# A routed expert layer on one core: routing by halves, one-hot matrices in batches, and later reads of the second matrices

## The reference

```python
w = weights[conditions]
y = jnp.einsum('bct,bcd->bdt', x, w)
probs = softmax(xt @ w_router)              # xt: y as (1024, 256), 16 experts
top_w, top_i = top_k(probs, 4);  top_w = top_w / sum(top_w)
g = silu(xt @ we1[e]) * (xt @ we3[e]) * cw[:, e]
moe_out = sum over e of g @ we2[e]
shared = silu(xt @ ws1) * (xt @ ws3) @ ws2
out = x + shared / 5 + moe_out * 4 / 5
```

## Time and profile before

| | us |
|---|---|
| median of 3 runs | 150.36 |
| lowest and highest | 146.83, 150.56 |
| the profiled execution | 146.87 |
| its span, first to last instruction | 145.0 |
| TensorE, VectorE, ScalarE, GpSimd busy | 133.6, 103.3, 78.9, 66.3 |

### The profile page before, as it was taken

The page is one execution under the profiler, slowest core; times in us unless marked ns, Lnnn a source line. Parts: engine busy times, 40 slices in busy tenths (PEclk is TensorE's granted clock), DMA queues, the critical chain, the costliest instruction groups (busy, mean ns, idle before and its releaser), DMA issues.

```text
span 145.0 us, 2785 instructions
## 1 busy us (share of the span) xinstructions
PE 133.6 (92%) x786; PEld 112.0 (77%) x786; DVE 103.3 (71%) x290; ACT 78.9 (54%) x193; POOL 66.3 (46%) x79
## 2 busy tenths in 40 slices
PE   5999999989798999999999999899999999999470
PEld 2347997778487788999898889798999888888350
DVE  1301879998828999877879887887888653066992
ACT  4003637999404986677586777447945321107900
POOL 0700000002765687778776566577777777000000
PEclk9999999999999999999999999999999999999998
DMA  2823898989952232365437322122222222399924
GB/s 43 288 60 80 239 255 291 341 250 285 368 189 75 77 98 83 112 183 181 152 107 204 124 101 92 66 113 109 109 106 87 101 109 112 85 392 411 374 77 145
DMA packets 17549, 24.18 MB, mean 167 GB/s; under 512 B 3424, under 2 KB 14304, under 8 KB 17408
## 3 DMA queue, kind: packets, MB, share of 16 engines
q1 hardware_dynamic: 13440, 14.23, 30.1%
q0 software_dynamic: 3120, 8.52, 16.6%
q10 hardware_dynamic: 976, 1.26, 2.6%
HBM read 17.58 MB, written 6.42 MB: 166 GB/s over the span
## 4 chain that ended last, share of the span: by engine, by line
PE 61%; DVE 21%; DMA 7%; issue 5%; ACT 3%; DVEq 1%; ACTq 0%
PE up_ps L1004 17%; PE down_ps L1022 11%; PE down_ps L920 8%; PE gate_ps L907 5%; PE up_ps L907 4%; PE up_ps L998 4%; PE gate_ps L957 4%; PE down_ps L982 3%; PE down_ps L862 2%; DMA itok_rows<-in_itok_B 2%; DMA g<-in_L_cond_weights,cond_idx 2%; DVE g L632 2%; ACT w_hi L468 2%; DVE raw L805 2%; DVE x_lo L764 2%
## 5 line engine op out<-in xcount | busy, mean ns | idle before, releaser
L444 POOL DMA_INDIRECT result<-store_t,back_i x32 | 31.3, 979 | 12.9 <-issue 6.7
L437 POOL DMA_INDIRECT xt<-y_of,token_i x16 | 16.3, 1019 | 35.0 <-DVE token_i L716 28.1
L798 DVE SCALAR_TENSOR_TENSOR store_t<-down_ps,valid,store_t 128x256 f32 x47 | 21.7, 461 | 8.7 <-DVE store_t L798 5.8
L1004 PE MATMUL up_ps<-w_hi,x_hi 128*128 x78 | 23.8, 305 | 1.1 <-DVE x_lo L764 0.9
L1022 PE MATMUL down_ps<-w,gt 128*128 x94 | 24.5, 381 | 0.0
L1004 PE MATMUL up_ps<-w_lo,x_hi 128*128 x78 | 22.1, 283 | 0.0
L1004 PE MATMUL up_ps<-w_hi,x_lo 128*128 x78 | 22.0, 282 | 0.0
L437 POOL DMA_INDIRECT raw<-y_of,token_i x16 | 15.8, 985 | 4.9 <-issue 4.0
L1022 PEld LDWEIGHTS down_ps<-w,gt 128*128 128x128 f32 x94 | 16.0, 190 | 1.7 <-issue 0.5
L1004 PEld LDWEIGHTS up_ps<-w_hi,x_hi 128*128 128x128 f32 x78 | 14.8, 190 | 2.5 <-issue 2.4
L764 DVE TENSOR_TENSOR x_lo<-store_t,x_hi 128x256 fp32r<-128x256 f32 x39 | 14.8, 421 | 0.6 <-ACT x_hi L536 0.3
(11 more groups left out here) (156 smaller groups left out, 260.0 us busy)
## 6 DMA issues: line engine op xcount, KB each, us to landing
raw<-in_L_ffn_we SPq DMA_DIRECT2D x30, 128.0 KB, 3.3
w<-in_L_ffn_we SPq DMA_DIRECT2D x4, 512.0 KB, 6.4
w_lo<-result SPq DMA_DIRECT2D x4, 512.0 KB, 6.7
raw<-result SPq DMA_DIRECT2D x4, 512.0 KB, 7.0
acc<-in_x SPq DMA_DIRECT2D x2, 512.0 KB, 4.6
y_of<-store_t ACTq DMA_DIRECT2D x1, 1024.0 KB, 6.0
out<-acc SPq DMA_DIRECT2D x3, 256.0 KB, 2.2
xt<-in_L_ffn_ws SPq DMA_DIRECT2D x4, 128.0 KB, 2.7
```

The lines of the kernel that those rows point to most:

```text
L437: pool.indirect_dma_start(rows_of(p)[:, j % 2, :], None, y_of, bass.IndirectOffsetOnAxis(ap=token_i[:, j:j + 1], axis=0),).then_inc(tile_i ...
L444: pool.indirect_dma_start(result, bass.IndirectOffsetOnAxis(ap=back_i[:, j:j + 1], axis=0), merged[:, j, :], None,).then_inc(result_out[j ...
L798: dve.scalar_tensor_tensor(out=into, in0=out_ps[n % 2][:, h, :], scalar=valid[:, it:it + 1], in1=into, op0=ALU.mult, op1=ALU.add).then_inc ...
L1004: last = pe.matmul(gu_ps[b][:, h, :], (x_hi, x_lo)[a][:, b, h, k * P:(k + 1) * P], pair_of(w, experts[h], k), start=(m == 0), stop=(m == 3 ...
```

## The change

1. **y's rows.** ScalarE copies y a second time as `y_f`, in float32, a piece at a time, between `y_hi` and the splits; `token_rows` turns these pieces back with 16 transposes.
2. **Routing by halves.** The searches and the comparison that makes `pick` are done per half, with `low(0)` in the first; `top_d` goes behind the mask, and its exponential on ScalarE behind three more splits. TensorE does a half gate product ahead of the ranks.
3. **One-hots.** `tile_hot`, `row_hot` and `dest_hot` are laid out with the pair's number n innermost, their inputs are bfloat16, and constants `count_tile`, `count_row` (1,024 elements each) and `count_n` are made at the start. `rows_hot` does one comparison of 1,024 elements in place of eight. `dest_hot` has two planes, not three: the partition (one copy on ScalarE) and n (one product on VectorE). `back_i` is made first, and `token_i` is its upper bits. The matmuls of `choices` have 64 columns and read both operands with a step.
4. **Second matrices.** SP waits for the first four gathers before it issues `w_2`; TensorE's wait for it moves from ahead of the first turn to the first product that reads it.

```diff
@@ views
+        y_f = store_t[:, 0:TT, :].rearrange("p t d -> p (t d)").rearrange("p (k n) -> p k n", k=KD)
-        row_hot = early(16, 8).bitcast(BF16).rearrange("p (n r) -> p n r", r=P)
-        tile_hot = early(24, 2).bitcast(BF16).rearrange("p (n j) -> p n j", j=TILES)
-        dest_hot = early(26, 6).bitcast(BF16).rearrange("p (n m j) -> p n m j", m=3, j=TILES)
+        row_hot = early(16, 8).bitcast(BF16).rearrange("p (c r n) -> p c r n", c=TOP_K, n=TT)
+        tile_hot = early(24, 2).bitcast(BF16).rearrange("p (j n) -> p j n", n=TK)
+        dest_hot = early(26, 4).bitcast(BF16).rearrange("p (m j n) -> p m j n", m=2, n=TK)
...
@@ sync
+            for j in range(2 * RING - 2):
+                sp.wait_ge(tile_in[j], 16)
             for q in range(4):
...
                 sp.dma_start(w_2[:, e, :], we2[e].rearrange("e h d -> h e d")).then_inc(w_2_in, 16)
@@ scalar
-            high(0)
-            high(1)
+            for h in range(2):
+                for k in range(KD):
+                    act.wait_ge(y_lo_done, KD * h + k + 1)
+                    act.activation(y_f[:, k, h * HALF:(h + 1) * HALF], y_ps[h][k][:, :], ACT.Copy).then_inc(y_f_done, 1)
+                high(h)
...
             for n in HI_ROWS:
                 high(n)
+            act.wait_ge(diff_done, 1)
+            act.activation(top_e[:, :, :], top_d[:, :, :], ACT.Exp).then_inc(exp_done, 1)
...
-                    act.activation(dest_hot[:, :, 0, :], tile_hot, ACT.Copy, scale=part[:, 0:1]).then_inc(dest_hot_done, 1)
-                    for k in range(TOP_K):
-                        act.activation(told[:, :, k, 2, :], hot[:, :, k, :], ACT.Copy, scale=float(k)).then_inc(dest_hot_done, 1)
-                    for t in range(TT):
-                        act.activation(told[:, t, :, 1, :], hot[:, t, :, :], ACT.Copy, scale=float(t)).then_inc(dest_hot_done, 1)
+                    act.activation(dest_hot[:, 0, :, :], tile_hot, ACT.Copy, scale=part[:, 0:1]).then_inc(dest_hot_done, 1)
@@ vector
-            step(dve.tensor_copy(count_r[:, :], count_w))
+            step(dve.tensor_copy(count_row, spread(count_w, TT)))
+            step(dve.tensor_copy(count_tile, spread(count_w[:, 0:TILES], TK)))
+            step(dve.tensor_copy(count_n, count_w[:, 0:TK]))
...
-            dve.tensor_tensor(tile_hot, repeat(count_i[:, 0:TILES], TK), spread(tile_i[:, :], TILES), ALU.is_equal).then_inc(tile_hot_done, 1)
-            chain(dve.tensor_copy(row_f[:, :], row_i[:, :]))
+            step(dve.tensor_copy(tile_f, tile_i[:, :]))
+            chain(dve.tensor_copy(row_f, row_i[:, :]))
+            dve.tensor_tensor(tile_hot, count_tile, repeat(tile_f, TILES), ALU.is_equal).then_inc(tile_hot_done, 1)
+            dve.wait_ge(tile_hot_done, 1)
+            dve.tensor_tensor(dest_hot[:, 1, :, :], tile_hot, repeat(count_n, TILES), ALU.mult).then_inc(dest_hot_done, 1)
...
             def rows_hot(c):
-                for n in range(TT * c, TT * c + TT):
-                    dve.tensor_scalar(row_hot[:, n, :], count_r[:, :], row_f[:, n:n + 1], None, ALU.is_equal).then_inc(row_hot_done, 1)
+                dve.tensor_tensor(row_hot[:, c, :, :], count_row, repeat(row_f[:, TT * c:TT * c + TT], P), ALU.is_equal).then_inc(row_hot_done, 1)
...
@@ tensor
             def token_rows(j):
+                if j % 2 == 0:
+                    pe.wait_ge(y_f_done, KD * (j // 2 + 1))
                 for i in range(2):
-                    last = pe.matmul(row_ps[j][:, i * D:(i + 1) * D], cond_bd[:, 2 * j + i, :], acc[:, 2 * j + i, :], start=True, stop=True)
+                    t = 2 * j + i
+                    for k in range(KD):
+                        last = pe.transpose(row_ps[j][:, i * D + k * P:i * D + (k + 1) * P], y_f[:, k, t * P:(t + 1) * P], ident[:, :])
...
-                    last = pe.matmul(dest_ps.rearrange("p m j -> p (m j)"), row_hot[:, n, :], dest_hot[:, n, :, :].rearrange("p m j -> p (m j)"),
+                    last = pe.matmul(dest_ps.rearrange("p m j -> p (m j)"), row_hot[:, c, :, i], dest_hot[:, :, :, n].rearrange("p m j -> p (m j)"),
                                      start=(n == 0), stop=(n == TK - 1))
...
+            pe.wait_ge(dve_lo, 1)
+            gate_up(0, 0, [0])
             ranks()
-            for s in range(2):
-                pe.wait_ge(dve_lo, 1)
-                if s == 1:
-                    pe.wait_ge(row_out, 4)
-                gate_up(s, 0)
-                gate_up(s, 1)
+            gate_up(0, 0, [1])
+            gate_up(0, 1)
+            pe.wait_ge(row_out, 4)
+            gate_up(1, 0)
+            gate_up(1, 1)
             pe.wait_ge(w_2_in, 16)
             down(0)
...
-            pe.wait_ge(w_2_in, 16 * 5)
             turn_pair(0)
...
+                    if n == 0:
+                        pe.wait_ge(w_2_in, 16 * 5)
```

More of the change, by code:

```diff
@@ L158, in adaln_ffn @@
         ones = small[:, 576:576 + P // 2].bitcast(BF16)
-        count_r = small[:, 640:640 + P // 2].bitcast(BF16)
+        count_n = small[:, 640:640 + TK // 2].bitcast(BF16)
         later = early(8, 2)
         tile_i, row_i = (later[:, k * TK:(k + 1) * TK].bitcast(I32) for k in range(2))
-        row_f, token_f = (later[:, k * TK:(k + 1) * TK] for k in range(2, 4))
+        row_f, tile_f = (later[:, k * TK:(k + 1) * TK].bitcast(BF16)[:, 0:TK] for k in range(2, 4))
+        place_f = early(10, 1)[:, 0:TK]
         parts = later[:, 128:128 + 4 * E].rearrange("p (m e) -> p m e", e=E)
@@ L223, in adaln_ffn @@
         row_out = sem("row_out")
+        y_f_done = sem("y_f_done")
         y_kept = sem("y_kept")
@@ L632, in gated @@
                 dve.tensor_tensor(g[:, h, :], sil[:, h, :], up_ps[h][:, :], ALU.mult).then_inc(g_done, 1)
-            low(0)
             for h in range(2):
@@ L643, in _ @@
                     step(dve.max(top_v[:, t, :], lg[:, t, :]))
-            dve.wait_ge(route, done[0])
-            dve.tensor_tensor(top_d[:, :, :], top_v[:, :, 0:TOP_K], top_v[:, :, 0:1].to_broadcast((P, TT, TOP_K)), ALU.subtract).then_inc(diff_done, 1)
-            for t in range(TT):
-                step(dve.max_index(top_i[:, t, :], top_v[:, t, :], lg[:, t, :]))
-            dve.wait_ge(route, done[0])
-            chain(dve.tensor_tensor(pick[:, :, :, :], count_i[:, 0:E].bitcast(U32).rearrange("p (a b e) -> p a b e", a=1, b=1).to_broadcast((P, TT, TOP_K, E)),
-                                    top_i[:, :, 0:TOP_K].rearrange("p t (k a) -> p t k a", a=1).to_broadcast((P, TT, TOP_K, E)), ALU.is_equal))
+                dve.wait_ge(route, done[0])
+                for t in range(TH * h, TH * h + TH):
+                    step(dve.max_index(top_i[:, t, :], top_v[:, t, :], lg[:, t, :]))
+                if h == 0:
+                    low(0)
+                dve.wait_ge(route, done[0])
+                step(dve.tensor_tensor(pick[:, r, :, :], count_i[:, 0:E].bitcast(U32).rearrange("p (a b e) -> p a b e", a=1, b=1).to_broadcast((P, TH, TOP_K, E)),
+                                       top_i[:, r, 0:TOP_K].rearrange("p t (k a) -> p t k a", a=1).to_broadcast((P, TH, TOP_K, E)), ALU.is_equal))
+            dve.wait_ge(route, done[0])
             with nc.allow_low_precision(reason="0 and 1 are exact in bfloat16"):
@@ L653, in _ @@
                 dve.tensor_tensor(mask[:, :, :], picks[:, :, 0, :], picks[:, :, 1, :], ALU.add).then_inc(mask_done, 1)
+            dve.tensor_tensor(top_d[:, :, :], top_v[:, :, 0:TOP_K], top_v[:, :, 0:1].to_broadcast((P, TT, TOP_K)), ALU.subtract).then_inc(diff_done, 1)
             low(1)
@@ L714, in _ @@
             dve.wait_ge(inverted, 1)
-            chain(dve.tensor_copy(token_f[:, :], dest_ps[:, 1, :]))
-            dve.scalar_tensor_tensor(out=token_i[:, :], in0=dest_ps[:, 0, :], scalar=float(TT), in1=token_f[:, :],
-                                     op0=ALU.mult, op1=ALU.add).then_inc(token_done, 1)
-            dve.wait_ge(token_done, 1)
-            dve.scalar_tensor_tensor(out=back_i[:, :], in0=token_i[:, :], scalar=float(TOP_K), in1=dest_ps[:, 2, :],
+            chain(dve.tensor_copy(place_f[:, :], dest_ps[:, 1, :]))
+            dve.scalar_tensor_tensor(out=back_i[:, :], in0=dest_ps[:, 0, :], scalar=float(TK), in1=place_f[:, :],
                                      op0=ALU.mult, op1=ALU.add).then_inc(back_done, 1)
+            dve.wait_ge(back_done, 1)
+            dve.tensor_scalar(token_i[:, :], back_i[:, :], 2, None, ALU.logical_shift_right).then_inc(token_done, 1)
             gated(1)
```

24 lines of the change are left out of this document (11 added, 13 removed).

## The result

The changed kernel takes 151.74 us, the median of four runs (150.37 to 152.29). Four runs of the kernel before on the same chip have a median of 148.7 us (146.83 to 150.56). The ratio is 1.0313, with a 95% interval of 1.0196 to 1.0430, so the change makes it slower; that it is by more than 2% is not quite shown. The ratio leaves out the two slow runs of before, 150.36 and 150.56 us; with all of them the medians differ by 2.0%, and e12_before_again shows what sets those runs apart. The forecast was 149.7 us and most likely no difference. The time lies inside the range given (145.8 to 151.9), but the median moved up and not down.

A forecast was written before the change was run, and what follows sets the result against it. It took one serial thread over VectorE and TensorE until 39.5 us, then TensorE's loop, as the bound. Routing -0.3 and comparisons -0.33 made -0.6 us, other terms 0: 150.36 to 149.7 us, range 145.8 to 151.9.

The forecast's parts named there:

- nothing in the profile tells where the other two spent 3.5 us more: Kernel before's runs: the profile did not explain why two took about 150.4 us and the lowest 146.83.
- rival B: Second matrices: runs near 150.4 us were late because the 2 MB landed late; the change removes that, median 146.3; chance 0.18.
- Carrying a difference of the profiled execution over to the median: Total time: the 0.6 us saving worked out on the profiled execution was taken off the median, 150.36 to 149.7 us.
- price on the thread: 0: y's rows by transposes: no cost on the serial critical chain, between -0.1 and +0.3 us; TensorE waits for the mask anyway.
- net -0.3: Routing by halves: mask 0.4 us earlier, top_d ahead of low(1) costs 0.1, so 0.3 us saved.
- Part 3, the comparisons: Batched one-hots on VectorE: 0.70 us per form of 1,024 elements, bringing gated(0) forward by a further 0.33 us.
- Rival C: Batched one-hots: VectorE takes them at one element a step, net +1.0 before gated(0), 151.7 us in all; chance 0.10.
- I take 0, by the row with a step: Inversion's 32 matmuls: strided reads cost nothing, since float32 weights with a step of 2 cost only 4% more.
- the bound of +4.6 us: Inversion's 32 matmuls: upper bound if every weight load is like a float32 one and no longer overlapped.
- Rival A: Inversion: TensorE reads strided one-hots slowly; 100 ns more per matmul gives 153.0 us, the bound 154.4; chance 0.22.
- price 0, cover 1.5 to 3 us: Later second matrices: no cost, the 2 MB landing 1.5 to 3 us before their first user on TensorE.
- The sum: Whole kernel: -0.3 and -0.33 make -0.6 us for gated(0), releasing what follows; 146.3 us profiled, 149.7 by the median.

The follow-up runs named there:

- e12_before_again: The kernel before, unedited, run again for a second trace: 150.11 and 150.14 us.
- e4: The kernel after with y's rows by matmuls again, one-hots interleaved in pairs of columns, and the second matrices issued early again: 147.64 us, 0.9930 of before.
- e8: The kernel after with one-hots interleaved in pairs of columns and the second matrices issued early again, transposes kept: 146.38 us, 0.9889 of before.
- e3: The kernel after with y's rows made by eight matmuls again, without the four copies and the transposes: 153.41 us, 1.0369 of before.
- e10: e8 with routing by halves undone (eight searches after both halves, one comparison of 512, ranks first): 146.26 us, 0.9906 of before.
- e5: The kernel after with pairs in row_hot alone (stationary operand step 2, moving operand step 32): 150.32 us, one execution.
- e2: The kernel after with one-hots interleaved only in pairs of columns ("the pairs"), so both matmul operands step by 2: 148.2 us, 1.0005 of before.
- e6: The kernel after with pairs in tile_hot and dest_hot alone (stationary operand step 8, moving operand step 2): 148.74 us, one execution.
- e1: The kernel after without SP's wait for four gathers, so the second matrices are issued early; TensorE's later wait stays: 150.24 us, 1.0162 of before.
- e9_ranks_first: e8 with the rank matmuls ahead of the half gate product again: 146.3 us, 0.984 of before.
- e11_warm_nine: e8 with one more 512-wide warm-up matmul in front of y (WARM = 9): 146.32 us, 0.9869 of before.

## Why the prediction was wrong, step by step

**The spread of the runs ("nothing in the profile tells where the other two spent 3.5 us more", and rival B).** It goes with TensorE's granted clock: among the runs of before beside e12, 146.8 to 147.0 us at 0.994 to 0.997 and 150.2 to 150.65 at 0.976 or 0.977. The profiled execution was one without a stretch at 0.50, and the rival that blamed a late load fell with e12: the wait it would have removed was not there. Carrying a difference of the profiled execution over to the median was a weak step, since at a granted clock of 0.50 (e12) the chain at 19 to 24 us runs over TensorE, and not over the VectorE rows on which the difference was worked out.

**Part 1, "price on the thread: 0".** Wrong, to the good side. The step behind it, that TensorE waited for the mask in the kernel before as well, was a misreading: its row matmuls ended as the mask was done. With those matmuls kept, the earlier mask and the gate half ahead of the ranks bring nothing, since TensorE comes late. Measured: e4 against e8 -1.3 us, e3 against after -1.7. The transposes are what lets part 2 count.

**Part 2, mask 0.4 us earlier, net -0.3.** Right at the full clock (mask 22.00, 0.5 earlier; e10 against e8 0.4 us). In the kernel after's own profile it is lost: the mask is done at 22.3, and TensorE comes to the ranks at 23.42.

**Part 3, the comparisons.** Right: 0.69 us per form against 0.70 forecast, and gated(0) 0.9 us earlier in e5 and e8 in all, against 0.6 forecast. Rival C (one element a step) fell.

**Part 3, the inversion: "I take 0, by the row with a step".** This is the step that failed. The row chosen had float32 weights with a step of two elements, and said nothing of a step of 8 or 32 bfloat16 elements. Worse, it was a row of weight loads, while the operand that cost most was the moving one (112 ns a matmul in e5, against 31 in e2), of which no row was looked at; the bound of +4.6 us, which held, was worked out from loads alone too. Measured: +2.3 us in the chain (3.70 for 1.39; with steps of 2 the new width is 0.4 under the old), +3.5 us in the median against the pairs. Rival A described it, with "100 ns more each" (measured 85 more than with steps of two), and at a chance of 0.22 it was underrated: a bound with 0 at one end and 4.6 at the other, on an operation that sits whole on the thread, gives no reason to take an end. The stationary operand cost less: 62 ns a matmul with a step of 8 (e6), 31 with a step of 2 (e2).

**Part 4, "price 0, cover 1.5 to 3 us".** This failed too. The cover was right for the one user that I looked at: the first product with a second matrix never waited. But the 2 MB moved from 32 us, where the first gathers met their end and none took over 4.8 us, to 44.74, where the next gathers share the DMA engines with them (share 1.10 over 47 to 53 us). One gather took 7.6 us and not 2.9, and the fourth turn waited. What was to be asked is who else uses the engines at the new place, not only who reads the bytes. Worth +1.5 (e1) to +1.8 us (e8 against e2) in the medians. The early place does not spare the gathers either, once they start earlier: in e8 the one issued at 35.72 us took 6.6 us. It was in time for the first turn at 42.29, which has no DMA wait. Slow gathers came with both places; part 4 put them where a turn had to wait for one.

**The sum.** From the kernel before's profiled execution, 146.9 us, to the kernel after's, 151.8, by the places in the traces: routing and comparisons -0.9 and the stretch at half the clock at 19 to 22 us +1.0 (gated(0) is at 28.84 in after and 27.88 in e5, the same program up to there but for the layout of one comparison), the inversion +2.3, the stretch at 36 to 39 us +0.2 (the first turn is 2.5 us late, the inversion's end 2.4), the late gather +2.1. That makes 4.7 of 4.9; the rest lies behind the loop and was not followed. e5, with no such stretch at all and an inversion of 3.57 us, took 150.3, 3.5 us over before at about the same clock (0.993 and 0.996). By the same places it is gated(0) -0.9, the inversion +2.2 and the gather +1.9.

What stays open is why the clock falls when it does. In one program it falls in some executions and not in others, beginning at 18 to 20.4 us in the traces that have it; the idle time ahead of y goes with it in thirteen traces of fourteen, and nothing was run that changes it alone. Whether the slow inversion brought the second fall at 36 us, which only the kernel after and e1 show of four traces with an inversion over 3.5 us, wasn't settled either.

## What to carry to other kernels

When a batched form on VectorE is bought with a stride for TensorE, look at both operands of each matmul, and interleave in pairs: VectorE's comparisons of 1,024 elements took 0.69 us with runs of two equal values as with runs of 8 and 32, and the matmul ran at 31 ns with a step of 2 elements, against 116 with steps of 8 and 32. When a large transfer moves, list what else is on the DMA engines at the new place, small gathers on the critical path first. And look at the granted clock of every run before taking a difference from one profile: here two executions of one kernel lie 3.2 us apart with it (150.11 us at 0.976, 146.87 at 0.996), more than most edits are worth.

The pairs with the second matrices read early (e8_pairs_early) are 1.1% faster than the kernel before (0.4 to 1.8%); e9_ranks_first, e10_no_halves and e11_warm_nine are as good, and their differences from it can't be told.

## What was not expected of the hardware

- A matmul of 64 columns in bfloat16: 31 ns with steps of 2 elements in both operands, 62 with a step of 8 in the stationary one, 112 with a step of 32 in the moving one, 116 with both.
- TensorE at half its clock (granted 0.50) for three to seven microseconds with the engine busy throughout, in some executions of a program and not in others: nine of fourteen traces have it beginning at 18 to 20.4 us, after the engine had been busy without a gap since about 12 us.
- A gather issued 3.5 us after the first of four loads of 0.5 MB took 7.6 us to land; the slowest in e2, e3, e5 and e6, which have the same order, took 6.0 to 8.2, where the median of the gathers is 2.9 to 3.2. With the loads at 32 us the slowest took 6.6 in e8 and 6.7 in e10, and no turn waited.
